# A selective-scan block with quantized FFN: transposes instead of diagonal matmuls for half of the scan inputs, and residual sums in SBUF

## What is computed

```python
# x: (16, 256, 128); 256 inner channels, 16 states, 4 taps
h = layernorm(x)
xz = h @ W_in + b_in;  x_in, z = split(xz)
xc = silu(causal_conv4(x_in) + conv_b)              # per channel
Bm, Cm = split(xc @ W_xp + b_xp)                    # 16 + 16 columns per token
delta = softplus(xc @ W_dt + b_dt)
# for every channel d and state s, over the 256 steps t:
#   state[t] = exp(delta[t,d] * A[d,s]) * state[t-1] + (delta[t,d] * xc[t,d]) * Bm[t,s]
#   y[t,d]   = sum_s state[t] * Cm[t,s]  + D_skip[d] * xc[t,d]
out = (y * silu(z)) @ W_out + b_out
x = x + layernorm(layernorm_alpha_beta(h + out))
h2 = layernorm(x)
# one scale for the whole of h2 and one for the weight, rounding to fp8 steps
x = x + layernorm(fp8(h2) @ fp8(W_ffn).T + bias)
```

## Time and profile before

| what | value |
|---|---|
| median of 3 runs | 634.68 us (633.74 to 635.59) |
| the profiled execution, its own time | 635.3 us |
| its span, first to last instruction | 633.6 us |
| start to the first unit | 33.1 us |
| slots 0 to 7 | to about 556 us |
| last sums and norms, and the tail | to the end |

### The profile page before, as it was taken

The page is one execution under the profiler, slowest core; times in us unless marked ns, Lnnn a source line. Parts: engine busy times, 40 slices in busy tenths (PEclk is TensorE's granted clock), DMA queues, the critical chain, the costliest instruction groups (busy, mean ns, idle before and its releaser), DMA issues.

```text
span 633.6 us, 10337 instructions
## 1 busy us (share of the span) xinstructions
PE 543.9 (86%) x2883; PEld 419.9 (66%) x2883; DVE 502.8 (79%) x1007; ACT 439.8 (69%) x884; POOL 299.9 (47%) x332
## 2 busy tenths in 40 slices
PE   6799999998999979998999889998999797861390
PEld 4467686877687857786787758786787576761130
DVE  4456688798988878798879977988979998984692
ACT  3449893989488946987498739894799676802273
POOL 3313262558263825565445716482646465401274
PEclk8979999999999999998999989998999999977555
DMA  7102451154305340346015601533043506520048
GB/s 192 41 1 42 92 103 31 35 100 91 60 18 117 68 85 1 74 80 129 1 34 99 141 12 25 108 74 75 1 96 70 117 1 129 105 51 0 17 42 92
DMA packets 23411, 41.95 MB, mean 66 GB/s; under 512 B 3777, under 2 KB 14145, under 8 KB 23361
## 3 DMA queue, kind: packets, MB, share of 16 engines
q0 software_dynamic: 13440, 35.66, 30.1%
q1 hardware_dynamic: 9920, 5.78, 3.5%
HBM read 3.68 MB, written 4.19 MB: 12 GB/s over the span
## 4 chain that ended last, share of the span: by engine, by line
PE 49%; DVE 16%; issue 13%; POOL 12%; ACT 6%; DMA 1%; DVEq 1%; POOLq 0%; ACTq 0%
PE drive L1007 20%; PE hT L1023 12%; DVE state L1224 6%; PE fbank L966 4%; PE fbank L948 3%; DVE acc_d L1247 3%; POOL u L495 2%; POOL ysumT L534 2%; POOL ysumT L532 2%; ACT decay L750 2%; PE bbank L1041 2%; PE fbank L955 2%; POOL state L631 1%; PE bbank L1033 1%; PE drive L948 1%
## 5 line engine op out<-in xcount | busy, mean ns | idle before, releaser
L1224 DVE TENSOR_TENSOR_SCAN state<-decay,drive 128x512 f32<-128x512 f32 x256 | 297.6, 1203 | 30.3 <-PE drive L1007 23.0
L1007 PE MATMUL drive<-diag,uT 128*128 128x256 f32 x1024 | 248.6, 387 | 0.8 <-DVE uT L1444 0.8
L750 ACT ACTIVATE decay<-delta,a_neg 128x510 f32<-128x510 f32 x256 | 170.7, 731 | 59.9 <-DVE state L1224 56.7
L1007 PEld LDWEIGHTS drive<-diag,uT 128*128 128x128 f32 x1024 | 189.2, 195 | 23.0 <-DVE uT L1444 1.0
L1023 PE MATMUL hT<-ident,state 128*128 128x128 f32 x1024 | 145.5, 281 | 25.2 <-DVE acc_d L1247 19.9
L1023 PEld LDWEIGHTS hT<-ident,state 128*128 128x128 f32 x1024 | 121.8, 145 | 57.2 <-issue 25.6
L507 POOL TENSOR_SCALAR_AFFINE_SELECT diag<-Bt 128x512 f32<-128x512 f32 x128 | 94.6, 743 | 75.4 <-PE drive L1007 62.4
L771 ACT ACTIVATE term<-hT,Ct 128x256 f32<-128x256 f32 x256 | 103.2, 486 | 7.4 <-PE hT L1023 7.3
L523 POOL DMA_DIRECT2D acc<-term x64 | 60.0, 938 | 26.7 <-DMA acc<-term 12.0
L1247 DVE SCALAR_TENSOR_TENSOR acc_d<-hT,Ct,acc_d 128x256 f32<-128x256 f32 x160 | 66.5, 469 | 6.1 <-PE hT L1023 6.0
L948 PE MATMUL fbank<-xnT,w_tap 128*128 128x512 f32 x112 | 51.6, 603 | 0.0
(11 more groups left out here) (176 smaller groups left out, 612.3 us busy)
## 6 DMA issues: line engine op xcount, KB each, us to landing
acc<-term POOLq DMA_DIRECT2D x64, 512.0 KB, 4.7
out_dram<-x_all SPq DMA_DIRECT2D x8, 256.0 KB, 2.4
out_dram<-term POOLq DMA_DIRECT2D x8, 256.0 KB, 5.4
x_all<-in_L_attn_x_dram SPq DMA_DIRECT2D x2, 256.0 KB, 3.9
state<-in_L_attn_conv_w_dram SPq DMA_DIRECT2D x1, 512.0 KB, 5.8
w_in<-in_L_attn_W_in_dram SPq DMA_DIRECT2D x1, 256.0 KB, 3.9
w_dt<-in_L_attn_W_dt_dram SPq DMA_DIRECT2D x1, 256.0 KB, 4.5
w_out<-in_L_attn_W_out_dram SPq DMA_DIRECT2D x1, 128.0 KB, 4.2
```

The lines of the kernel that those rows point to most:

```text
L750: last = nc.scalar.activation(decay[:, g % DECAYS, h, :, s, 1:], delta[:, par, h, :, 1:], ACT.Exp, scale=a_neg[:, h, SG * g + s:SG * g + s ...
L1007: last = nc.tensor.matmul(dst[:, :, P * c:P * c + P], uT[:, par, TC * b + c, P * h:P * h + P], diag[:, n % DIAGS, c, :, :], start=True, st ...
L1224: nc.vector.tensor_tensor_scan(state[:, n % STATES, h, :, :].rearrange("p s t -> p (s t)"), decay[:, g % DECAYS, h, b, :, :].rearrange("p ...
```

## The change

It has these parts:

1. For the units in `MUL_U` (2, 4, 6, 8, 9, 11, 13, 15, the same in every pair) POOL does not write diagonals. `scale_u` multiplies uT by B elementwise (one tensor_tensor of 128x1024 elements in two chunks, two states and 256 channels) into `scaled`, two buffers of its own, and PE transposes the product, eight 128x128 transposes per unit, into the same `drive`. `scale_u` needs uT, and the buffer that the second `MUL_U` unit before it has left.
2. The tables of places have new numbers on four engines.
3. In the tail, POOL's accumulating DMA adds `fn` of groups 0 to 5 to x_all in SBUF, for group 6 POOL adds by tensor_tensor, and group 7 is worked in halves: ACT norms and POOL adds the first, DVE norms and adds the second, whose matmul result has a bank of its own. SP then writes x_all to DRAM, group after group. The SP writes of the loop and the DMAs that add in DRAM are gone.
4. Buffers: `ysumT` is gone (the sum is made in acc), `pre` is the same memory as `dt_v`.

```diff
+FN = 4
+ADDED = PAIRS - 2
+MUL_U = (2, 4, 6, 8, 9, 11, 13, 15)
-PE_STEPS = dict(front_in=(0, 6, 15, 21), front_transpose=(23,), front_dt=(24, 28), front_bc=(37,),
-                front_ut=(40, 41), back_y=(12, 14), back_out=(19,), back_transpose=(45,))
-DVE_STEPS = dict(front_stats=(1,), front_shift=(1,), front_low=(19,), front_bc=(25,), front_delta=(24,),
-                 back_y=(8, 9), back_norms=(12, 13, 17, 21, 24, 27, 27), back_amax=(31,))
+PE_STEPS = dict(front_in=(0, 6, 18, 21), front_transpose=(22,), front_dt=(24, 28), front_bc=(36,),
+                front_ut=(41, 45), back_y=(13, 14), back_out=(18,), back_transpose=(45,))
+DVE_STEPS = dict(front_stats=(1,), front_shift=(7,), front_low=(18,), front_bc=(25,), front_delta=(24,),
+                 back_y=(8, 8), back_norms=(12, 13, 17, 20, 24, 27, 28), back_amax=(31,))
...
-            with sp.Fori(0, PAIRS // 2) as i:
-                for par in range(2):
-                    pr = Pair(i * 2 + par, par)
-                    sp.wait_ge(b_sum, nth(pr, 1, 1))
-                    sp.dma_start(out_v[:, bass.ds(pr.v * CH, CH), :], x_k[:, bass.ds(pr.v * CH, CH), :]).then_inc(x1_stored, 16)
+            for g in range(PAIRS - 1):
+                if g < ADDED:
+                    sp.wait_ge(added[g % FN], 16 * (g // FN + 1))
+                else:
+                    sp.wait_ge(f_sum, 1)
+                sp.dma_start(out_v[:, CH * g:CH * g + CH, :], x_k[:, CH * g:CH * g + CH, :]).then_inc(stored, 16)
+            for k, part_done in enumerate((f_sum_late, f_sum_early)):
+                first = CH * (PAIRS - 1) + CH // 2 * (1 - k)
+                sp.wait_ge(part_done, 1)
+                sp.dma_start(out_v[:, first:first + CH // 2, :], x_k[:, first:first + CH // 2, :]).then_inc(stored, 16)
...
+            def scale_u(pr, par, n):
+
+                g, b, j = n // PAIR, n % PAIR, MUL_U.index(n)
+                pool.wait_ge(bc_ready, nth(pr, 3, 2))
+                pool.wait_ge(uT_ready, nth(pr, 2, 2))
+                old = trailing(pr, par, j, 2, len(MUL_U))
+                if old:
+                    pool.wait_ge(drive_ready, nth(old[0], 2 * UNITS, 2 * MUL_U[old[2]] + 2))
+                u_t = uT[:, par, TC * b:TC * b + TC, :].unsqueeze(2).to_broadcast([P, TC, SG, DI])
+                b_t = Bt[:, par, g, b, :, :].unsqueeze(3).to_broadcast([P, TC, SG, DI])
+                nc.gpsimd.tensor_tensor(scaled[:, j % 2, :, :, :], u_t, b_t, ALU.mult).then_inc(diag_ready, 1)
...
-                pool.dma_start(out_v[:, CH * grp.v:CH * grp.v + CH, :], chunks(fn[:, grp.v % 4, :]), accum_op=ALU.add)\
-                    .then_inc(stored[grp.v % 4], 16)
+                x_g = x_all[:, TOK * grp.v:TOK * grp.v + TOK]
+                if grp.v < ADDED:
+                    pool.dma_start(x_g, fn[:, grp.v % FN, :], accum_op=ALU.add).then_inc(added[grp.v % FN], 16)
+                elif grp.v == ADDED:
+                    nc.gpsimd.tensor_tensor(x_g, x_g, fn[:, grp.v % FN, :], ALU.add).then_inc(f_sum, 1)
+                else:
+                    half_g = x_all[:, TOK * grp.v:TOK * grp.v + TOK // 2]
+                    nc.gpsimd.tensor_tensor(half_g, half_g, fn[:, grp.v % FN, 0:TOK // 2], ALU.add).then_inc(f_sum_early, 1)
...
                     for c in range(TC):
+                        if n in MUL_U:
+                            for s in range(SG):
+                                last = nc.tensor.transpose(dst[:, s, P * c:P * c + P],
+                                                           scaled[:, MUL_U.index(n) % 2, c, s, P * h:P * h + P], ident[:, :])
+                            continue
                         last = nc.tensor.matmul(dst[:, :, P * c:P * c + P], uT[:, par, TC * b + c, P * h:P * h + P],
                                                 diag[:, n % DIAGS, c, :, :], start=True, stop=True)
```

More of the change, by code:

```diff
@@ L198, in build_sandwich @@
         dt_v = sb("dt_v", [P, HALVES, TOK])
+        pre = dt_v
         dt_e = sb("dt_e", [P, HALVES, TOK])
@@ L208, in build_sandwich @@
         diag = sb("diag", [P, DIAGS, TC, SG, P])
+        scaled = sb("scaled", [P, 2, TC, SG, DI])
         state = sb("state", [P, STATES, HALVES, SG, L])
@@ L360, in build_sandwich @@
         f_norm = sem("f_norm")
-        x1_stored = sem("x1_stored")
-        stored = [sem("added_%d" % k) for k in range(4)]
+        f_sum = sem("f_sum")
+        f_sum_early = sem("f_sum_early")
+        f_sum_late = sem("f_sum_late")
+        f_late = sem("f_late")
+        added = [sem("added_%d" % k) for k in range(FN)]
+        stored = sem("stored")
         x_v = x.rearrange("b l d -> (b l) d").rearrange("(k p) d -> p k d", p=P)
@@ L878, in last_norm @@
                 act.wait_ge(f_shift, nth(grp, 1, 1))
-                if grp.after(4):
-                    act.wait_ge(stored[grp.v % 4], 16 * (grp.v // 4))
-                for j in range(CH):
-                    last = nc.scalar.activation(fn[:, grp.v % 4, DM * j:DM * j + DM],
-                                                f_bank(grp.v)[:, DM * j:DM * j + DM],
+                if grp.after(FN):
+                    act.wait_ge(added[grp.v % FN], 16 * (grp.v // FN))
+                for j in range(CH // 2 if is_last(grp) else CH):
+                    last = nc.scalar.activation(fn[:, grp.v % FN, DM * j:DM * j + DM],
+                                                f_chunk(grp.v, j),
                                                 ACT.Identity, bias=fshift[:, par, j:j + 1],
@@ L1163, in tail @@
                     pe.wait_ge(f_norm, grp.v - 3)
-                nc.tensor.matmul(f_bank(grp.v).rearrange("p (j d) -> p j d", d=DM), ones_row[:, :],
-                                 bias_g[0:1, :].unsqueeze(1).to_broadcast([1, CH, DM]), start=True, stop=False)
+                parts = 2 if is_last(grp) else 1
+                for k in range(parts):
+                    bank = hT[:, 0, :] if k else f_bank(grp.v)
+                    nc.tensor.matmul(bank[:, 0:TOK // parts].rearrange("p (j d) -> p j d", d=DM), ones_row[:, :],
+                                     bias_g[0:1, :].unsqueeze(1).to_broadcast([1, CH // parts, DM]), start=True, stop=False)
                 pe.wait_ge(xq_ready, nth(grp, 1, 1))
                 for j in range(CH):
-                    last = nc.tensor.matmul(f_bank(grp.v)[:, DM * j:DM * j + DM], xq[:, par, P * j:P * j + P],
-                                            wqT_g[:, :], start=False, stop=(j == CH - 1))
+                    last = nc.tensor.matmul(f_chunk(grp.v, j), xq[:, par, P * j:P * j + P],
+                                            wqT_g[:, :], start=False,
+                                            stop=(j == CH - 1 or is_last(grp) and j == CH // 2 - 1))
                 last.then_inc(f_full, 1)
@@ L1547, in _ @@
             in_turn(tail, range(PAIRS + 2))
+            last_par, buf = (PAIRS - 1) % 2, (PAIRS - 1) % FN
+            late = fn[:, buf, TOK // 2:]
+            dve.wait_ge(f_shift, PAIRS)
+            dve.wait_ge(added[buf], 16 * ((PAIRS - 1) // FN))
+            for j in range(CH // 2, CH):
+                nc.vector.tensor_scalar(fn[:, buf, DM * j:DM * j + DM], f_chunk(PAIRS - 1, j),
+                                        frstd[:, last_par, j:j + 1], fshift[:, last_par, j:j + 1], ALU.mult, ALU.add)\
+                    .then_inc(f_late, 1)
+            dve.wait_ge(f_late, CH // 2)
+            x_late = x_all[:, PAIRS * TOK - TOK // 2:PAIRS * TOK]
+            nc.vector.tensor_tensor(x_late, x_late, late, ALU.add).then_inc(f_sum_late, 1)
 _INS = ['L0_attn_x', 'L0_attn_W_in', 'L0_attn_b_in', 'L0_attn_conv_w', 'L0_attn_conv_b', 'L0_attn_W_xp',
```

45 lines of the change are left out of this document (23 added, 22 removed).

## The result

| kernel | median, us | ratio to before, 95% interval |
|---|---|---|
| before, beside it on the same chip | 635.13 | |
| the change | 615.12 (614.71 to 617.69) | 0.970 [0.967, 0.973] |

The change is 20.0 us faster; the forecast was 28 and 607. The profiled execution took 615.11 us with a span of 613.4.

The account below looks back on a forecast made before the run. The loop was taken to wait on the handing over between PE and DVE, both nearly full; 24.6 (six pairs) - 3 (clock) + 3.5 + 1 (slots 0, 7) + 1.7 (end) = 27.8 us off 635.3, forecast 607 us, range 588 to 624.

Parts of the forecast that it names:

- The likeliest case: Whole kernel: a pair of sequences takes near 64 us, forecast 607 us, 598 to 614; chance 0.5.
- POOL's product: POOL in the loop: 2.36 us per product, 13 us more per pair, costed at nothing on the path.
- PE's drives: PE in the loop: eight transposes take 0.87 us for a drive's 1.73, saving 6.9 us of PE's queue per pair.
- DVE's waits: DVE in the loop: 6.5 us of waits go and 2.4 come, a net gain of 4.1 us per pair.
- the drive's wait: DVE, unit 6's scan waiting for its drive: 1.06 us per pair goes.
- wait for the transposes behind the first projection: DVE in the loop: 1.71 us per pair goes because PE arrives earlier.
- The clock: PE in the loop, mostly units 12 to 15: three more falls of the granted clock, 3 us lost.
- the third rival: PE's clock in the loop falls and stays down, about 700 us at half the queue slowed; chance 0.04.
- The end: Last norms and final DMAs: finish at 628.5 instead of 630.2, 1.7 us won, between 0 and 3.5.
- Slots 0 and 7: First and last slots, outside the full pairs: 3.5 us won in slot 0 and 1 in slot 7.
- The limits named: Prediction wrong if a pair takes under 61.5 or over 66.5 us, PE's clock is 0.50 over a tenth, or PE waits for `scaled`.
- The second rival: Loop: ACT or POOL takes the wait over, a pair gains near 2 us, 620 us in all; chance 0.2.

Follow-up runs that it names:

- `filled`: The changed kernel with 16 spare identity transposes on PE in unit 15, ahead of the transposes of h2, where PE stood idle: 610.93 us, ratio 0.965.
- `only_end`: The kernel before with the new end and new buffers alone, no products and places as before: 631.75 us, ratio 0.995.

## Why the prediction was right, and where it was off

The sign, the range (588 to 624) and most of the mechanism held. The likeliest case was too good by 8 us.

- **POOL's product**: at nothing on the path, as forecast. It is cheaper than its nearest row, 1.93 us for 2.36. But it was only free because of the places. "The other moves of places I cost at nothing, because DVE's scans cover them" is the step that failed here: at the old places the same products cost 6.3 us, and the four moves that end the collisions bring 6.7 back. The trace of before shows no collision for these three instructions; the section of the Trainium skill cited above would have given me the rival.
- **PE's drives**: 0.87 us a set, exact. PE never waited for `scaled`.
- **DVE's waits**: both roots gone (1.15 and 1.16), the second y 0.75 for 0.7, the residual down 0.9. Mis-sized: the drive's wait kept half of its 1.06, and `front_low` 1.2 for 1.7.
- **"The wait for the transposes behind the first projection, 1.71 ... : PE arrives earlier"** is the failed step of the sum. PE arrives earlier, and then waits 1.9 to 2.3 us for ACT's uT, after which its clock is 0.50; the wait is 2.18. The row stood at two of the loop's five turns before, not at all of them, and `filled` shows that 1.67 of the 2.18 are the clock's, not the queue's. The step booked 6 x 1.71 = 10.3 us of gain; at the three turns without a jump the change lost 3.1.
- **DVE's jump back** was in no step. It costs 4.7 us for 3.1 before, 3.2 over two jumps, because the product of unit 2 stands ahead of the last accumulating DMA and moves its traffic into the fetch. The forecast read a slot without a jump; the scan at 369.81 us, which waits 3.08, is in none of its rows. Together the turns explain 10.3 + 6.3 = 16.6 us against the forecast; 3 of them were booked as the clock's, and the rest of the loop came out 1.6 us better than forecast: 12 us.
- **The clock**: three more falls were forecast, from idle time in units 12 to 15. The idle time is there, in unit 15, but the low clock lies over the turn behind it; the loop and its last turn have six falls where there were four, two more and not three, and their price is in the 3.1. The loop's granted clock is 0.97 as before, so the third rival is out. By the Trainium skill's rule on transposes (TensorE: Matmul & The Clock Gate, Part 4: PE-mode transpose) half of the drives no longer count. This loop speaks against the rule, though other matmuls stand between; the earlier trace rows speak against it more plainly.
- **The end**: 3.8 for 1.7 by the traces and 3.4 by `only_end`, about the 3.5 given as the most. By its own terms the step's sum is 628.9 and not 628.5 (624.7, four times 0.45, 2.4), which makes its gain 1.3. SP's last issue came 2.1 us behind ACT's last norm, not 3. **Slots 0 and 7** gave 5.3 for 4.5. The first 1.5 us, ahead of the first unit, stay unexplained.
- **The limits named**: a pair took 66.6 us in that window, just over the 66.5 at which the forecast called itself wrong, and 65.5 as the mean of the six periods, against 67.1 before. The second rival (620) came nearer to the time than the forecast, 5 us against 8, but not by its mechanism: ACT and POOL took nothing over but the 1.2 us of dt_v. That 607 was only 8 us off is partly luck: a gain of 10.3 us that did not come and 6.3 us of loss in no step or with the wrong sign stand against 3 booked for the clock and some 6 us that the rest gave beyond the forecast.

## What to carry to other kernels

Where two engines are both nearly full, a shorter queue on the one and moved steps on the other are one change: price them together, not as a sum. Read the slot in which the loop jumps back apart from the others, and look what DMA traffic stands before it; writing out the loop of DVE alone gave 15.7 us here, for two jumps. Before GpSimd gets long instructions, list VectorE's instructions that have all operands in SBUF, and keep them apart in time.
